# A RoPE attention and two local-attention layers on one core: the norm's factor and offset move from the weights into ScalarE's copies, and the layer weights are prepared in pieces in earlier passes

## The chip, the cores and the metric

The kernel runs on one core of one Trainium2 chip. The metric is the device time of one execution in microseconds (us). The engines are TensorE (PE, with its weight loads as PEld), VectorE (DVE), ScalarE (ACT), GpSimd (POOL) and SyncE (SP), which here only issues transfers. Each works through its own list of instructions in order and waits on semaphores of the others.

## The reference

x has 8 batches of 512 tokens and 256 features. Its parts, cut to what matters:

```
xn = layernorm(x)                               # no factor, no offset
s  = softmax(causal(rope(xn Wq) rope(xn Wk)^T / 16)) (xn Wv)
for l in (0, 1):                                # on xn
    h = shift_token(x)                          # second half of the features, one token later
    q, k, v = split(h @ wqkv[l])                # 256 -> 3 x 512, 8 heads of 64
    q, k = l2norm(q) * qs, l2norm(k) * ks       # then rotary with xpos scales
    x = x + local_attention(q, k, v, window 128) @ wo[l]
    h = shift_token(x)
    h = (h - mean) / sqrt(var + 1e-5) * g[l] + b[l]
    a, gate = split(h @ w1[l] + b1[l])          # 256 -> 2 x 682
    x = x + (a * gelu(gate)) @ w2[l] + b2[l]
out = x_in + s * silu(x)
```

## The kernel before

All products are made of fp32r parts: a number is written as hi (what ACT's copy rounds it to) and lo (the rest, a subtraction on DVE or POOL), and a product is three: hi·hi, hi·lo, lo·hi. So weights must be prepared: class `W` holds for wqkv, w1, wo and w2 a staging buffer, a `_hi` and a `_lo`, and functions `high_*` (ACT) and `low_*`. In the kernel before, the norm's factor g is multiplied into w1 when hi and lo are made (`high_w1`, `low_w1`), and the offset b goes through w1 in `b1_products`, 44 one-column products on PE, whose sum `b1_columns` adds to the bias b1.

`attention_block` does the first attention in 9 software-pipelined steps: step i projects and rotates batch i (front) and does softmax and values of batch i−1 (back). Steps 1 to 6 are one hardware loop; 0, 7 and 8 are written out, and step 8 has only the back. The queue of SP loads batch i+1 (L309), stores the result of the step (L314), loads the layers' weights but w1 in step 0 and w1 in step 7, into the room of the rotation tables `a_tables`. In step 8 ACT and DVE prepare layer 0's weights (L149 to L189), POOL scales the layers' rotation tables (L329) and PE does `b1_products` (L197). L210 is the end of the block, at which all engines meet.

`layers_block` has 17 passes. Pass i does the attention part of one batch and the feed-forward part (ffn) of the batch before: pass 0 attention only, 1 to 7 in layer 0, 8 the turn (attention in layer 1, ffn in layer 0), 9 to 15 in layer 1, 16 ffn and the final products with x and s. The order of the work in a pass is written out by hand for each engine. PE projects four tiles of q, k, v (L1245) with the norm's mean and variance between them (L1252, L1256), then alternates products of the hidden layer (`hidden`, L1271) with transposes of q and k (L1293), then scores (L1310), transposes of the weights (L1324), values (L1340), `down` (L1281) and the output product (L1358). ACT squares projected tiles (L876), makes the inverse norms (L881, L883), f_hi (`high_f`, L962), gelu (L910) and the exponentials (L943). DVE rotates (L1048, L1054), sums squares (L1058, L1060), multiplies the gate (L1068), copies k's transposes out of PSUM (`k_evac`, L1124) and makes maxima (L1104); it adds the attention's result to x at the end (L1222) and starts the norm (L1228, L1229). POOL makes f_lo (`low_f`, L834), the squares and scaled tiles (L812, L819) and h_lo (L823).

In the turn, layer 1's weights are prepared: wqkv at the end of pass 7, the rest in pass 8, with `b1_products` at unit 9 of its attention; PE waits for all low parts of wqkv at the start of pass 8 and for the others at its end.

## Time and profile before

| | |
|---|---|
| time, median of 3 runs | 1464.69 us (1464.49 to 1465.24) |
| profiled execution | 1466.16 us, span of instructions 1464.4 us |
| granted clock of TensorE, mean | 0.983 |
| PE busy | 1397.7 us, 95% |
| DVE / ACT / POOL busy | 66% / 58% / 52% |
| chain that ended last | PE 72%, ACT 6%, issue 3% |

The stretches, read from the windows: start and steps of the attention block to 191.3 us, its last step and end to 216.8, pass 0 to 280.4, passes 1 to 6 to 729.1, pass 7 to 804.8, pass 8 to 891.2, passes 9 to 15 to 1415.1, pass 16 to 1464.4. A time in a row is in us from the span's start; the number behind it is the length, and brackets at a row's end give how long the engine was idle before and what released it.

### The profile page before, as it was taken

The page shows a single profiled execution, that of the slowest core. Times are in us where ns is not written, and L with a number is a line of the kernel's source. Part 1 is how long each engine was busy: PE and PEld are TensorE (multiplying, and loading weights), DVE is VectorE, ACT ScalarE, POOL GpSimd, SP SyncE. Part 2 cuts the span into 40 slices and gives each one's busy share as a digit, 9 for nine tenths or more (in the row PEclk, how much of TensorE's full clock was granted, in tenths as well). Part 3 has the DMA queues.
Part 4 walks back from the last instruction along what each step waited for, and adds up shares of the span by engine and source line. Part 5 has one row for each costly group of instructions (what it writes and reads, how often), then busy time and mean ns, then how long its engine had stood idle before and what let it go on. Part 6 is the DMA issues. An engine that isn't in the chain of part 4 may idle for free.

```text
span 1464.4 us, 24262 instructions
## 1 busy us (share of the span) xinstructions
PE 1397.7 (95%) x7828; PEld 1066.0 (73%) x7828; DVE 961.4 (66%) x2664; ACT 853.1 (58%) x2175; POOL 754.2 (52%) x514
## 2 busy tenths in 40 slices
PE   5999978999999999999999999999999999999987
PEld 5778766677777777777776767777777777777766
DVE  5767657666666666667576767676766666666666
ACT  3555555564646465656566574747474747565763
POOL 2333336383837373737474643747373738383810
PEclk9999989999999999999999999999999999999998
DMA  7111020000000000000001010000000000000037
GB/s 213 30 57 52 20 68 1 1 1 1 0 0 0 0 0 0 0 0 0 0 1 46 14 59 1 1 0 0 0 0 0 0 0 0 0 0 0 0 106 238
DMA packets 35239, 33.28 MB, mean 23 GB/s; under 512 B 8364, under 2 KB 32896, under 8 KB 35200
## 3 DMA queue, kind: packets, MB, share of 16 engines
q1 hardware_dynamic: 35200, 32.79, 7.0%
q8 instruction: 21, 0.34, 0.1%
q14 instruction: 18, 0.15, 0.0%
HBM read 24.39 MB, written 8.39 MB: 22 GB/s over the span
## 4 chain that ended last, share of the span: by engine, by line
PE 72%; ACT 6%; issue 3%; DVE 1%; POOL 1%; DMA 1%; ACTq 0%; SPq 0%; DVEq 0%; POOLq 0%
PE l_psF L1271 9%; PE l_ring L1245 9%; PE l_psP L1245 9%; PE l_ring L1271 7%; PE l_ring L1340 7%; PE l_psP L1324 7%; PE l_psF L1358 6%; PE l_psS L1281 5%; ACT l_att L943 4%; PE l_psS L1293 4%; PE l_psF L1310 4%; PE l_ring L1281 2%; PE l_psS L1310 2%; PE l_psF L1252 1%; PE l_psF L1256 1%
## 5 line engine op out<-in xcount | busy, mean ns | idle before, releaser
L812 POOL TENSOR_TENSOR l_att<-l_att 128x1024 f32<-128x1024 f32 x64 | 154.1, 2408 | 322.6 <-DVE l_att L1054 322.6
L859 POOL TENSOR_TENSOR l_att<-l_att,l_rinv 128x1024 f32<-128x1024 f32 x64 | 121.2, 1894 | 66.9 <-DVE l_rinv L1111 66.0
L923 ACT ACTIVATE l_att<-l_psP 128x384 f32<-128x384 f32 (+1 forms) x128 | 70.2, 548 | 130.5 <-PE l_psP L1324 130.5
L828 POOL TENSOR_TENSOR l_u_lo<-l_att,l_u_hi 128x512 fp32r<-128x512 f32 x90 | 115.4, 1291 | 58.2 <-ACT l_u_hi L918 58.2
L1116 DVE COPY l_att<-l_psP 128x384 f32<-128x384 f32 (+1 forms) x128 | 78.8, 616 | 85.5 <-PE l_psP L1324 85.2
L1324 PE MATMUL l_psP<-ident,l_att 128*128 128x128 f32 x896 | 125.2, 280 | 2.2 <-DVE l_att L1116 1.5
L1324 PEld LDWEIGHTS l_psP<-ident,l_att 128*128 128x128 f32 x896 | 99.2, 142 | 32.1 <-issue 30.0
L819 POOL TENSOR_TENSOR l_att<-l_att,l_rn 128x1024 f32<-128x1024 f32 x64 | 121.6, 1913 | 0.0
L943 ACT ACTIVATE l_att<-l_psF,l_nb 128x256 f32<-128x256 f32 x256 | 117.8, 483 | 0.0
L1104 DVE CUSTOM_DVE_ANT_0 l_psF<-l_psF,w_mask 128x256 f32<-128x256 f32 x256 | 101.0, 455 | 24.2 <-issue 24.2
L1340 PE MATMUL l_ring<-l_att 128*64 128x256 f32 (+1 forms) x1024 | 111.5, 360 | 1.4 <-ACT l_att L923 1.4
L943 ACT ACTIVATE l_att<-l_psS,l_nb 128x128 f32<-128x128 f32 (+1 forms) x256 | 104.6, 431 | 3.2 <-DVE l_nb L1104 2.8
L1340 PEld LDWEIGHTS l_ring<-l_att 128*64 128x64 f32 x1024 | 68.2, 137 | 51.7 <-issue 17.6
L1068 DVE SCALAR_TENSOR_TENSOR l_att<-l_psF,w_b,l_att 128x512 f32<-128x512 f32 x45 | 33.8, 750 | 108.2 <-ACT l_att L910 108.2
L1104 DVE CUSTOM_DVE_ANT_0 l_psS<-l_psS,w_mask 128x128 f32<-128x128 f32 (+1 forms) x256 | 83.4, 386 | 19.6 <-issue 19.6
L876 ACT ACTIVATE l_att<-l_ring 128x512 f32<-128x512 f32 x64 | 38.1, 596 | 96.6 <-PE l_ring L1245 96.6
L340 POOL TENSOR_TENSOR a_t<-a_raw,a_tables 128x256 f32<-128x256 f32 x32 | 29.4, 917 | 121.9 <-ACT a_raw L355 121.9
L1245 PE MATMUL l_psP<-w_wq_hi,l_hhi 128*128 128x512 f32 x192 | 87.8, 457 | 0.0
L1245 PE MATMUL l_ring<-w_wq_hi,l_hhi 128*128 128x512 f32 x192 | 77.0, 401 | 7.6 <-POOL l_hlo L823 6.6
L1271 PE MATMUL l_psF<-l_fhi,w_w_hi 128*128 128x512 f32 x192 | 80.7, 421 | 0.0
L1310 PE MATMUL l_psF<-l_att 64*128 64x256 f32 x512 | 71.5, 398 | 9.6 <-ACT l_att L943 9.3
L1058 DVE TENSOR_REDUCE l_ssq<-l_att 128x16 f32<-128x1024 f32 x64 | 77.2, 1206 | 0.0
(203 smaller groups left out, 4064.3 us busy)
## 6 DMA issues: line engine op xcount, KB each, us to landing
a_tables<-in_x SPq DMA_DIRECT2D x8, 512.0 KB, 4.2
scratch_s<-a_o SPq DMA_DIRECT2D x8, 512.0 KB, 3.0
l_att<-in_x SPq DMA_DIRECT2D x8, 512.0 KB, 8.7
l_att<-scratch_s SPq DMA_DIRECT2D x8, 512.0 KB, 9.7
out_dram<-l_att SPq DMA_DIRECT2D x7, 512.0 KB, 6.3
aw_stage<-in_wqkv SPq DMA_DIRECT2D x2, 768.0 KB, 7.5
l_att<-in_wqkv SPq DMA_DIRECT2D x2, 768.0 KB, 5.2
w_w_raw<-in_w SPq DMA_DIRECT2D x2, 640.0 KB
```

The lines of the kernel that those rows point to most:

```text
L812: pool.tensor_tensor(rot[:, t, :], rot[:, t, :], t2[t % 2], ALU.add).then_inc(S["added"], 1)
L819: pool.tensor_tensor(r, r, along(rn[:, t, :], DH), ALU.mult).then_inc(S["rot_done"], 1)
L828: pool.tensor_tensor(U_lo[0:rows, j, :], gate_of(j, attn)[0:rows, :], U_hi[0:rows, j, :].bitcast(F32), ALU.subtract).then_inc(S["u_lo"], 1)
L859: pool.tensor_tensor(pr, pr, along(inv, 2 * P), ALU.mult).then_inc(S["p_done"], 1)
L943: last = act.activation(Pr[u % 3][:, g * 2 * P + c0:(g + 1) * 2 * P], ps[:, g * 2 * P + c0:(g + 1) * 2 * P], ACT.Exp, bias=nb[:, u % 3, g: ...
L1104: last = dve.tensor_tensor_reduce(out=block, in0=block, in1=maskT[:, c0:2 * P], scale=1.0, scalar=3e38, op0=ALU.add, op1=ALU.min, accum_ou ...
L1245: last = pe.matmul(proj_of[(3 * t + c) % 4], a[:, k, t * P:(t + 1) * P], w[:, k, c * INNER:(c + 1) * INNER], start=(m == 0), stop=(m == 3 ...
L1271: last = pe.matmul(hidden_of[j % 2][bank], w[:, k, tile * P:(tile + 1) * P], a[:, k, :], start=(m == 0), stop=(m == 3 * KD - 1))
L1281: last = pe.matmul(down_of[c], w[:, k, c * P:(c + 1) * P], u[:, k, :], start=(k == 0 and m == 0), stop=(k == HT - 1 and m == 2))
L1310: last = pe.matmul(ps[:, par * 512 + tt * 2 * P + c0:par * 512 + (tt + 1) * 2 * P], QT[rows, pair, t * P:(t + 1) * P], KT[rows, pair, max( ...
L1324: last = pe.transpose(psP[:, dst:dst + P], Pr[u % 3][:, src:src + P], ident[:, :])
L1340: last = pe.matmul(ring[pair % 2][rows, t * P:t * P + w], V[:, t, h * DH:(h + 1) * DH], PT[:, par, t * 2 * P:t * 2 * P + w], start=(t == 0 ...
```

## The change

- The norm's factor and offset are no longer in the weights. ACT makes f_hi in two Identity instructions of 128x512 with a factor and an offset per partition (`high_f`), and two more write the same value over its input in place (`affine`), from which f_lo is subtracted. `b1_products` and `b1_columns` are gone; b1 is loaded where it is used.
- In `hidden(i, 0)` the eight products that need f_hi alone come first, for both tiles, and the four with f_lo behind them. In the other calls the f_lo products are the last two of each tile.
- Layer 0's w1 has a buffer of its own and is loaded in step 0 with wqkv, both ahead of w2. wqkv is prepared in three pieces in step 6, w1 and wo in step 7, w2 in step 8; high parts on ACT, low parts of wqkv and w1 on DVE, of wo and w2 on POOL. POOL's table products (L329) move from step 8 to step 6, which is written out.
- In the turn wqkv is prepared in three pieces by columns, `high_wo` and `low_wo` at units 4 and 5, `low_w1` behind the last `o_low`, `low_w2` behind the start of the norm. PE waits for a part where it first uses it.

```diff
-    def high_wqkv(self, act, layer, stage, k):
-        act.wait_ge(self.S[f"wq_in{k}"], 16 * (layer + 1))
-        act.activation(self.wq_hi[:, k, :], stage[:, k, :], ACT.Copy).then_inc(self.S["wq_hi"], 1)
+    def high_wqkv(self, act, layer, stage, c):
+        for k in range(KD):
+            act.wait_ge(self.S[f"wq_in{k}"], 16 * (layer + 1))
+        cols = slice(c * INNER, (c + 1) * INNER)
+        act.activation(self.wq_hi[:, :, cols], stage[:, :, cols], ACT.Copy).then_inc(self.S["wq_hi"], 1)
 
     def high_w1(self, act, layer, stage, k):
         act.wait_ge(self.S["w1_in"], 64 * (layer + 1))
-        act.wait_ge(self.S["small"], self.SMALL)
-        act.activation(self.w1_hi[:, k, :], stage[:, k, :], ACT.Copy, scale=self.gcol[:, layer, k:k + 1]).then_inc(self.S["w1_hi"], 1)
-
-
-    def low_wqkv(self, dve, layer, stage, k):
-        dve.wait_ge(self.S["wq_hi"], KD * layer + k + 1)
-        dve.tensor_tensor(self.wq_lo[:, k, :], stage[:, k, :], self.wq_hi[:, k, :].bitcast(F32), ALU.subtract).then_inc(self.S["wq_lo"], 1)
+        act.activation(self.w1_hi[:, k, :], stage[:, k, :], ACT.Copy).then_inc(self.S["w1_hi"], 1)
+
+
+    def low_wqkv(self, dve, layer, stage, c):
+        dve.wait_ge(self.S["wq_hi"], 3 * layer + c + 1)
+        cols = slice(c * INNER, (c + 1) * INNER)
+        dve.tensor_tensor(self.wq_lo[:, :, cols], stage[:, :, cols], self.wq_hi[:, :, cols].bitcast(F32), ALU.subtract).then_inc(self.S["wq_lo"], 1)
 
     def low_w1(self, dve, layer, stage, k):
         dve.wait_ge(self.S["w1_hi"], KD * layer + k + 1)
-        dve.scalar_tensor_tensor(out=self.w1_lo[:, k, :], in0=stage[:, k, :], scalar=self.gcol[:, layer, k:k + 1],
-                                 in1=self.w1_hi[:, k, :].bitcast(F32), op0=ALU.mult, op1=ALU.subtract).then_inc(self.S["w1_lo"], 1)
-
+        dve.tensor_tensor(self.w1_lo[:, k, :], stage[:, k, :], self.w1_hi[:, k, :].bitcast(F32), ALU.subtract).then_inc(self.S["w1_lo"], 1)
...
-            with e.Fori(1, B - 1) as i:
+            with e.Fori(1, B - 2) as i:
                 step(i, True, True)
+            step(B - 2, True, True)
             step(B - 1, True, True)
             step(B, False, True)
...
+                sp.wait_ge(S["w_tr"], 3)
+                W.load_wqkv(sp, 0, stage_q)
+                W.load_w1(sp, 0, stage1)
                 sp.wait_ge(WS["w2pad"], 1)
                 W.load_w2(sp, 0)
-                sp.wait_ge(S["w_tr"], 3)
-                W.load_wqkv(sp, 0, stage_q)
...
-                if isinstance(i, int) and i == B - 1:
-                    W.load_w1(sp, 0, stage1)
...
-                else:
+                if isinstance(i, int) and i == B - 2:
                     layer_tables()
+                if isinstance(i, int) and i == B - 1:
+                    W.low_wo(pool, 0)
+                if isinstance(i, int) and i == B:
+                    W.low_w2(pool, 0)
...
+            def prepare(i, part):
+
+                if isinstance(i, int) and i == B - 2:
+                    W.high_wqkv(act, 0, stage_q, part)
+                if isinstance(i, int) and i == B - 1:
+                    if part < KD:
+                        W.high_w1(act, 0, stage1, part)
+                    else:
+                        W.high_wo(act, 0)
+                if isinstance(i, int) and i == B and part == 0:
+                    W.high_w2(act, 0)
...
-                if not front:
-                    W.high_wqkv(act, 0, stage_q, 1)
+                prepare(i, 0)
...
-                if not front:
-                    for k in range(KD):
-                        W.high_w1(act, 0, stage1, k)
-                    W.high_wo(act, 0)
-                    W.high_w2(act, 0)
...
-                if not front:
-                    for k in range(KD):
-                        W.low_wqkv(dve, 0, stage_q, k)
+                if front:
+                    rotate(i, 2)
+                    rotate(i, 3)
+                if isinstance(i, int) and i == B - 2:
+                    for c in range(3):
+                        W.low_wqkv(dve, 0, stage_q, c)
+                if isinstance(i, int) and i == B - 1:
                     for k in range(KD):
                         W.low_w1(dve, 0, stage1, k)
-                    W.low_wo(dve, 0)
-                    W.low_w2(dve, 0)
-                    W.b1_columns(dve, 0, psT)
-                if front:
-                    rotate(i, 2)
-                    rotate(i, 3)
...
-                if not front:
-                    W.b1_products(pe, 0, stage1, psT)
...
                 def low_f():
-                    ge(pool, S["f_hi"], i)
+                    ge(pool, S["affine_done"], i)
                     pool.tensor_tensor(flo[:, :, :], dF, fhi[:, :, :].bitcast(F32), ALU.subtract).then_inc(S["f_lo"], 1)
...
                 def high_f():
                     ge(act, S["hn_done"], i)
-                    act.activation(fhi[:, :, :], dF, ACT.Copy).then_inc(S["f_hi"], 1)
+                    for k in range(KD):
+                        last = act.activation(fhi[:, k, :], dF[:, k], ACT.Identity, scale=W.gcol[:, lf, k:k + 1], bias=W.bcol[:, lf, k:k + 1])
+                    last.then_inc(S["f_hi"], 1)
+
+                def affine():
+                    for k in range(KD):
+                        last = act.activation(dF[:, k], dF[:, k], ACT.Identity, scale=W.gcol[:, lf, k:k + 1], bias=W.bcol[:, lf, k:k + 1])
+                    last.then_inc(S["affine_done"], 1)
...
-                    if turn and j == TT:
-                        W.high_wo(act, 1)
...
+                        if turn and u == 4:
+                            W.high_wo(act, 1)
                         if turn and UNITS <= u < UNITS + KD:
                             W.high_w1(act, 1, stage1, u - UNITS)
                         if last and u == UNITS + 3:
-                            for k in range(KD):
-                                W.high_wqkv(act, 1, stage, k)
+                            for c in range(3):
+                                W.high_wqkv(act, 1, stage, c)
...
-                    W.low_wo(dve, 1)
...
-                        if turn and UNITS <= u < UNITS + KD:
-                            W.low_w1(dve, 1, stage1, u - UNITS)
+                        if turn and u == 5:
+                            W.low_wo(dve, 1)
...
                 if last:
+                    for c in range(3):
+                        W.low_wqkv(dve, 1, stage, c)
+                if turn:
                     for k in range(KD):
-                        W.low_wqkv(dve, 1, stage, k)
-                if turn:
-                    W.low_w2(dve, 1)
+                        W.low_w1(dve, 1, stage1, k)
                 if attn:
                     ge(dve, S["wo_ps"], i + 1)
                     for k in range(KD):
                         xk = xT[:, bass.ds(i - B * la, 1), k * X1:k * X1 + N]
                         dve.tensor_tensor(xk, xk, psF[:, k * N:(k + 1) * N].unsqueeze(1), ALU.add).then_inc(S["x_attn"], 1)
-                    if turn:
-
-                        W.b1_columns(dve, 1, psS[:, N:2 * N])
                     ge(dve, S["x_attn"], KD * (i + 1))
                     h = h_view(xT, i - B * la)
                     dve.tensor_tensor(rstdF[:, :].unsqueeze(1), h[:, 0:1, :], h[:, 1:2, :], ALU.add).then_inc(S["h_sum"], 1)
                     dve.tensor_scalar(dF, h, 1.0, None, ALU.mult).then_inc(S["h_ready"], 1)
+                if turn:
+                    W.low_w2(dve, 1)
...
                     m, of = 0, 3 * t + c - 4
+                    if fresh is not None:
+                        pe.wait_ge(WS["wq_lo"], 3 * fresh + c + 1)
...
             def hidden(i, j, attn):
                 u = i - 1
-                ge(pe, S["f_lo"], i)
+                ge(pe, S["f_hi"], i)
...
+                terms = [(k, w, fhi) for k in range(KD) for w in (w1_hi, w1_lo)] + [(k, w1_hi, flo) for k in range(KD)]
                 tiles = ((HFULL + j, 0), (j, 1)) if j < HFULL else ((2 * HFULL, 0),)
-                for tile, bank in tiles:
-                    m = 0
-                    for k in range(KD):
-                        for w, a in ((w1_hi, fhi), (w1_lo, fhi), (w1_hi, flo)):
-                            last = pe.matmul(hidden_of[j % 2][bank], w[:, k, tile * P:(tile + 1) * P], a[:, k, :], start=(m == 0), stop=(m == 3 * KD - 1))
-                            m += 1
+                for wanted in (("hi", "lo") if j == 0 else ("hi lo",)):
+                    if wanted != "hi":
+                        ge(pe, S["f_lo"], i)
+                    for tile, bank in tiles:
+                        for n, (k, w, a) in enumerate(terms):
+                            if ("lo" if a is flo else "hi") in wanted:
+                                last = pe.matmul(hidden_of[j % 2][bank], w[:, k, tile * P:(tile + 1) * P], a[:, k, :],
+                                                 start=(n == 0), stop=(n == 3 * KD - 1))
...
-                if turn:
-                    pe.wait_ge(WS["wq_lo"], KD * LAYERS)
-                if attn:
-                    project(i, 0)
+                if attn:
+                    project(i, 0, la if turn or not ffn else None)
...
+                if ffn:
+                    pe.wait_ge(WS["w1_lo"], KD * (lf + 1))
...
+                    pe.wait_ge(WS["w2_lo"], lf + 1)
...
-                        if turn and u == UNITS + 1:
-                            W.b1_products(pe, 1, stage1, psS[:, N:2 * N])
-                    if turn:
-                        pe.wait_ge(WS["wo_lo"], LAYERS)
+                    pe.wait_ge(WS["wo_lo"], la + 1)
                     output(i, range(0, 1))
                     values(i, PAIRS - 1, ffn)
                     output(i, range(1, PAIRS))
-                    if turn:
-                        pe.wait_ge(WS["w1_lo"], KD * LAYERS)
-                        pe.wait_ge(WS["w2_lo"], LAYERS)
```

ACT in an ordinary pass, from the third projected tile on. Before (L892 copies v, L962 is `high_f`, L876 squares the fourth tile):

```order
L892 ACTIVATE l_att<-l_ring 128x512
L962 ACTIVATE l_fhi<-l_ffn 128x1024
L41 ISA
L876 ACTIVATE l_att<-l_ring 128x512
L881 ACTIVATE l_lnq<-l_lnq 128x16
L883 ACTIVATE l_rn<-l_lnq 128x16
L41 REGISTER_ALU
```

And now (L951 is `high_f`, L956 `affine`):

```order
L880 ACTIVATE l_att<-l_ring 128x512
L951 ACTIVATE l_fhi<-l_ffn,w_b,w_g 128x512 x2
L956 ACTIVATE l_ffn<-l_ffn,w_b,w_g 128x512 x2
L41 ISA
L864 ACTIVATE l_att<-l_ring 128x512
L869 ACTIVATE l_lnq<-l_lnq 128x16
L871 ACTIVATE l_rn<-l_lnq 128x16
L41 REGISTER_ALU
```

Between the copy of v and the fourth square stand four instructions where one stood.

DVE at the end of step 6 and the beginning of step 7, now (L486 and L489 rotate, L160 is `low_wqkv`, L494 takes maxima, L479 and L480 write the low part and the copy of x):

```order
L486 TENSOR_TENSOR a_rot<-a_raw,a_tables 128x512
L489 TENSOR_TENSOR a_rot<-a_rot,a_t 128x512
L486 TENSOR_TENSOR a_rot<-a_raw,a_tables 128x512
L489 TENSOR_TENSOR a_rot<-a_rot,a_t 128x512
L160 TENSOR_TENSOR w_wq_lo<-aw_stage,w_wq_hi 128x2x512 x3
L494 TENSOR_REDUCE a_nb<-a_psS 128x1
L479 TENSOR_TENSOR a_hlo<-a_ring,a_hhi 128x512 x2
L480 COPY xT<-a_ring 128x512
L494 TENSOR_REDUCE a_nb<-a_psS 128x1
```

Before, the rotations of the loop's last step were followed by the maxima, and DVE's preparation stood at the very end of the block:

```order
L500 RECIPROCAL a_rinv<-a_sums 128x1
L505 COPY a_pt<-a_psP 128x512
L159 TENSOR_TENSOR w_wq_lo<-aw_stage,w_wq_hi 128x1536 x2
L163 SCALAR_TENSOR_TENSOR w_w_lo<-a_tables,w_g,w_w_hi 128x1408 x2
L173 TENSOR_TENSOR w_wo_lo<-w_wo_raw,w_wo_hi 128x1024
L189 TENSOR_TENSOR w_w_lo<-w_w_raw,w_w_hi 128x1536
L202 TENSOR_TENSOR w_b<-a_psT,w_b1raw 128x11
```

POOL now, in step 6 and step 7 (L327 and L328 are its part of the rotation, L316 the table products, L172 `low_wo`, L188 `low_w2`):

```order
L327 TENSOR_TENSOR a_t<-a_raw,a_tables 128x256
L328 TENSOR_TENSOR a_t<-a_raw,a_tables 128x256
L316 TENSOR_TENSOR w_cos<-w_cos,a_scl 128x512
L316 TENSOR_TENSOR w_sin<-w_sin,a_scls 128x512
L316 TENSOR_TENSOR w_cos<-w_cos,a_scl 128x512
L316 TENSOR_TENSOR w_sin<-w_sin,a_scls 128x512
L327 TENSOR_TENSOR a_t<-a_raw,a_tables 128x256
L328 TENSOR_TENSOR a_t<-a_raw,a_tables 128x256
```

The table products stood behind the last such pair of step 7 before; now they stand between those of step 6 and step 7.

DVE at the end of pass 8, before (L163 is `low_w1`, L189 `low_w2`, L202 `b1_columns`):

```order
L163 SCALAR_TENSOR_TENSOR w_w_lo<-l_ffn,w_g,w_w_hi 128x1408
L1116 COPY l_att<-l_psP 128x512
L1120 TENSOR_TENSOR l_ot_lo<-l_ring,l_ot_hi 128x512
L1083 SCALAR_TENSOR_TENSOR xT<-l_psS,w_b,xT 128x512
L1120 TENSOR_TENSOR l_ot_lo<-l_ring,l_ot_hi 128x512
L189 TENSOR_TENSOR w_w_lo<-w_w_raw,w_w_hi 128x1280
L189 TENSOR_TENSOR w_w_lo<-w_w_raw,w_w_hi 42x256
L1222 TENSOR_TENSOR xT<-xT,l_psF 128x512 x2
L202 TENSOR_TENSOR w_b<-l_psS,w_b1raw 128x11
L1228 TENSOR_TENSOR l_ffn<-xT 128x512
L1229 TENSOR_SCALAR l_ffn<-xT 128x1024
```

And now (L164 is `low_w1`, L188 `low_w2`):

```order
L1117 TENSOR_TENSOR l_ot_lo<-l_ring,l_ot_hi 128x512
L1080 SCALAR_TENSOR_TENSOR xT<-l_psS,w_b,xT 128x512
L1117 TENSOR_TENSOR l_ot_lo<-l_ring,l_ot_hi 128x512
L164 TENSOR_TENSOR w_w_lo<-l_ffn,w_w_hi 128x1408 x2
L1219 TENSOR_TENSOR xT<-xT,l_psF 128x512 x2
L1222 TENSOR_TENSOR l_ffn<-xT 128x512
L1223 TENSOR_SCALAR l_ffn<-xT 128x1024
L188 TENSOR_TENSOR w_w_lo<-w_w_raw,w_w_hi 128x1280
L188 TENSOR_TENSOR w_w_lo<-w_w_raw,w_w_hi 42x256
```

The two of w1 moved from among the units to directly before the addition to x, and those of w2 from before it to behind the start of the norm.

## Rows read from the trace of the kernel before

**Rows 1.** The page: busy time of each engine.

```profile
PE 1397.7 (95%) x7828; PEld 1066.0 (73%) x7828; DVE 961.4 (66%) x2664; ACT 853.1 (58%) x2175; POOL 754.2 (52%) x514
```

**Rows 2.** Windows: stretch, length, busy by engine, granted clock, DMA share, GB/s.

```profile
280.40:729.10 448.70, 442.74 (x2510) 334.31 (x2509) 293.53 (x870) 269.45 (x714) 259.13 (x168) 1.00 0.00 0
729.10:804.80 75.70, 73.69 (x418) 55.32 (x417) 52.20 (x148) 47.50 (x121) 43.18 (x28) 1.00 0.06 22
804.80:891.20 86.40, 83.41 (x463) 64.72 (x463) 56.05 (x151) 49.99 (x124) 43.48 (x28) 0.94 0.10 31
```

**Rows 3.** Chain of waits of one ordinary pass: start, length, what.

```profile
376.73 0.87 PE l_psS L1293 x8
...
380.40 0.91 PE l_psS L1293 x8
```

**Rows 4.** Timeline of ACT in that pass: start, length, instruction, [idle before].

```profile
370.08 1.05 ACT L962 ACTIVATE l_fhi<-l_ffn 128x1024 fp32r<-128x1024 f32 x1
...
371.03 0.58 ACT L876 ACTIVATE l_att<-l_ring 128x512 f32<-128x512 f32 x1
```

**Rows 5.** Timeline of DVE in that pass.

```profile
355.40 1.28 DVE L1222 TENSOR_TENSOR xT<-xT,l_psF 128x512 f32 x2 [3.17 <-PE l_psF L1358]
...
372.70 0.69 DVE L1048 TENSOR_TENSOR l_att<-l_ring,w_cos 128x512 f32<-128x512 f32 x1
...
376.47 0.19 DVE L1060 TENSOR_REDUCE l_lnq<-l_ssq 128x16 f32<-128x32 f32 x1
...
379.86 0.68 DVE L1124 COPY l_att<-l_psS 128x512 f32<-128x512 f32 x1
```

**Rows 6.** Timeline of POOL in that pass.

```profile
371.21 2.41 POOL L834 TENSOR_TENSOR l_flo<-l_ffn,l_fhi 128x1024 fp32r<-128x1024 f32 x1 [0.56 <-ACT l_fhi L962]
...
380.15 3.79 POOL L819 TENSOR_TENSOR l_att<-l_att,l_rn 128x1024 f32<-128x1024 f32 x2
```

**Rows 7.** Groups by form on ACT: busy us, mean ns of one.

```profile
L956 ACT ACTIVATE l_ffn<-l_psF,eps 128x512 f32<-128x512 f32 x16 | 11.0, 688 | 4.1 <-PE l_psF L1256 4.1
...
L958 ACT ACTIVATE l_psF<-l_ffn 128x512 f32<-128x512 f32 x16 | 9.6, 602 | 0.5
...
L918 ACT ACTIVATE l_u_hi<-l_att 128x512 fp32r<-128x512 f32 x75 | 46.7, 622 | 0.4
```

**Rows 8.** Windows around the arrival of x(2).

```profile
28.00:36.00 8.00, 7.96 (x50) 7.67 (x50) 2.85 (x5) 4.59 (x10) 2.52 (x2) 0.73 0.99 357
```

**Rows 9.** Timeline of DVE and of PE where attention step 6 ends and 7 begins.

```profile
165.43 0.69 DVE L491 TENSOR_TENSOR a_rot<-a_rot,a_t 128x512 f32<-128x512 f32 x1
...
170.49 0.29 DVE L496 TENSOR_REDUCE a_nb<-a_psS 128x1 f32<-128x128 f32 x1 [4.37 <-PE a_psS L619]
...
171.89 0.68 DVE L482 COPY xT<-a_ring 128x512 f32<-128x512 f32 x1
...
173.02 0.48 PE L600 MATMUL a_ring<-aw_hi,a_hhi 128*128 128x512 f32 x1
```

**Rows 10.** Timeline of DVE and of POOL at the end of step 7.

```profile
187.67 1.66 DVE L491 TENSOR_TENSOR a_rot<-a_rot,a_t 128x512 f32<-128x512 f32 x1
...
191.67 1.26 POOL L329 TENSOR_TENSOR w_sin<-w_sin,a_scls 128x512 f32<-128x512 f32 x1
```

**Rows 11.** Timeline of PE, and SyncE's waits, at the attention block's end.

```profile
203.50 6.70 PE L197 MATMUL a_psT<-w_b,a_tables 128*128 128x1 f32 x44
...
SPq L210 <- PEq L210: 4.8, 1, 4.8
```

**Rows 12.** Timeline of PE and of DVE in pass 8.

```profile
873.11 7.23 PE L197 MATMUL l_psS<-w_b,l_ffn 128*128 128x1 f32 x44
...
889.01 1.82 DVE L189 TENSOR_TENSOR w_w_lo<-w_w_raw,w_w_hi 128x1280 fp32r<-128x1280 f32 x2 [0.77 <-ACT w_w_hi L183]
```

**Rows 13.** Timeline of DVE and of PE in the last pass.

```profile
1429.21 1.22 DVE L1155 TENSOR_TENSOR l_flo<-l_ffn,l_fhi 128x1024 fp32r<-128x1024 f32 x1 [1.12 <-ACT l_fhi L962]
...
1429.81 1.09 PE L1350 MATMUL l_psP<-ident,xT 128*128 128x128 f32 x4 [3.13 <-ACT xT L928]
```

47 lines of the change are left out of this document (15 added, 32 removed).

## The prediction

> **What bounds the kernel now.** I read the page first: TensorE (PE) is busy for 95% of the span [rows 1], so time comes only from shortening the stretches in which it is not, or from PE work that goes away. The windows then say where those are [rows 2]. Six ordinary passes of the layers take 448.70 us, 74.78 each, at granted clock 1.00, with PE busy but for 1 us a pass. Pass 7 takes 75.70 and pass 8, in which the layer changes, 86.40 at a mean clock of 0.94: together 162.1 where two ordinary passes take 149.6, so the turn costs 12.5. The third place is the end of the attention block, where 44 one-column products take 6.70 and the block closes after them [rows 11].
>
> The chain of an ordinary pass is nearly all PE, so the question for each edit there is how much room the engines beside it have. I followed the place where the new ScalarE (ACT) work goes. There ACT writes f_hi (L962), then squares the fourth projection tile (L876) [rows 4]; VectorE (DVE) has by then worked without a gap since 355.40 and takes that square up at 372.70, goes on without a gap to the reduction at 376.47, behind which ACT does a logarithm, an exponential, a table load and the first gelu; DVE multiplies with it and then copies k's first bank, 379.86 to 380.54 [rows 4, 5]. PE's second block of transposes, which writes that bank again from its middle on, takes 0.91 where the block before took 0.87 [rows 3]. So this side chain ends just in time: PE already waits a few hundredths for it. A delay of its head has no slack behind it, only the one in front of it.
>
> **The norm's factor and offset.** f_hi was one copy of 128x1024 and becomes two Identity instructions of 128x512 with two pointer operands, with two more behind them (in place, for f_lo). All four stand ahead of the square. Successive instructions overlap by 0.10 (1.05 long, next one 0.95 later [rows 4]). The same shape costs 0.60 without a pointer and 0.69 with one, a plain copy in SBUF 0.62 [rows 7]. No row has two pointers. Bounds: the second costs nothing (pitch 0.62 + 0.09 − 0.10 = 0.61) or as much as the first (0.70). I take 0.70, since the only measured step is that of one more pointer. Then the square starts at 370.08 + 4 × 0.70 = 372.88, ends 0.58 later, and DVE begins at about 373.50 instead of 372.70: 0.80 late. As the chain behind has no slack, the pass grows by 0.80. With 0.61 the square ends at 373.10 and the delay is 0.44 (0.40 without the handover). Passes 1 to 7 and 10 to 15 are of this kind: **13 × 0.80 = +10.4** (low end +5.7). The new order of the first hidden products (eight that need f_hi alone, then four with f_lo) takes away no wait: f_lo starts about 1.8 later (373.0 instead of 371.21 [rows 6]) and ends at 375.4, when those four come up.
>
> The Trainium skill bears on the missing row (ScalarE: Activation LUTs, What ACT_TABLE_LOAD costs): an ACTIVATE takes 186 ns plus 0.833 per column, about 93 more for each [128,1] pointer operand, and neighbours overlap by about 93. The rows agree for one pointer (602 to 688 [rows 7]); no row here shows the second. By the page the pitch is an estimated 0.70 and the sum stays; were the second free, it would be 4.7 lower.
>
> The last pass has no projection to hide behind. There PE waits 3.13 for ACT's copies of xT behind f_hi [rows 13]. The four instructions take 2.80 where one took 0.95: **+1.85**.
>
> **The turn.** Gone are the 44 products in pass 8 (7.23 [rows 12]), the half-speed products that followed them, the wait for all of wqkv's low parts at the pass's start, and low_wo, which held DVE's maxima back. I take the whole excess: **−12.5**, the low end being the products alone, −7.2. Against this: pass 8 has the 0.80 too, and DVE enters it late, because PE no longer waits for low_wqkv but DVE still does it first; the two delays overlap on ACT, and I take **+1.05** for both. low_wo at the sixth unit: 0.05. In pass 8 DVE now does low_w1 in the 3.17 that it idles before adding to x [rows 5]: twice 1.22 × 1408/1024 [rows 13], 3.4, hidden but for 0.2. Behind the norm's first copies it does low_w2, 1.82 for its two instructions [rows 12], ahead of the first rotation of pass 9; DVE has no gap from there, so pass 9 is later by that, with the variance's chain in front: **+1.87**, in place of its 0.80.
>
> **The attention block.** Step 6's end gets POOL's four table products and DVE's three pieces of low_wqkv. DVE is free from 166.12 (165.43 + 0.69) to 170.49 [rows 9], and a 128x1024 subtraction takes 1.22 alone [rows 13], so three would take 3.66 and fit. But POOL reads SBUF at the same time. In step 7 of before a DVE rotation beside these very table products took 1.66 [rows 10] instead of 0.69 [rows 9], and POOL's product 1.26 when alone [rows 10], 1.3 with its start. If they alternate, three of POOL's lie between DVE's: 166.12 + 3.66 + 3.9 = 173.7, so the maxima of step 7 start 3.2 late, and with them the low parts and the copy of x at 171.89, on which PE's first projection waits; that copy ended at 172.57 and the projection came at 173.02 [rows 9], so 0.4 is slack: **+2.8**, from 0 (no alternation) to 3.5.
>
> The Trainium skill says the same of the port (SBUF — State Buffer, Who interferes with whom): a DVE instruction with two SBUF inputs and a GpSimd instruction that reads SBUF lock each other out for a whole instruction. The trace agrees (1.66 for 0.69). Without the lock the sum would be 2.8 lower.
>
> At step 7's end low_wo on POOL meets the last rotations in the same way: **+0.9** (a rotation grew by 0.97 [rows 9, 10]). ACT, busy for 58% of the span [rows 1], gets up to three copies a step there, and I count them as hidden between its evacuations. In step 8 high_w2 and low_w2 lie beside PE's work. At the close, SyncE last waits 4.8 for PE [rows 11], before that for the store; with the 44 products gone the store decides: **−4.8**. At the start 1.4 MB of w1 now go ahead of x(2), 3.9 us at the 357 GB/s of that stretch [rows 8]; x(2) was in before its use by about that much: **+0.1**, at most 1.5.
>
> **Sum:** 0.1 + 2.8 + 0.9 − 4.8 + 10.4 − 12.5 + 1.05 + 0.05 + 1.87 + 1.85 = +1.7. Against the profiled execution, 1466.16 with a span of 1464.4, that is 1467.9; the median of the three timed runs is 1464.69, so the time is forecast as **1466.4**. A measurement of this kernel can tell some 0.2%, 2.9 us, from no change; this is the same.
>
> **Rivals.**
> - *The second pointer is free.* Nothing in the trace is against it. 13 passes at 0.44, the last pass at 1.5: 1466.4 − 4.7 − 0.4 = 1461.3, and less if low_f lands sooner. 15 in 100.
> - *The square's delay is covered.* If PE's wait at the transposes is not DVE's, or the delay is caught up between reduction and gelu, the passes cost nothing: −10.4, 1456. For it: that wait is only 0.04. Against it: no gap on DVE and ACT from the square to the copy. 12 in 100.
> - *The lock doesn't alternate.* DVE's three pieces run back to back: 1466.4 − 2.8 = 1463.6. 10 in 100.
> - *Slower: POOL's chain becomes the bound.* All of POOL's products behind f_lo move by 1.8. The third scaled tile ends at 380.15 + 1.9 = 382.1 [rows 6], so at 383.9 after, and the third block of transposes comes at 384.0 plus PE's own delay of 0.8. Under 0.9 of slack decides; each 0.3 over it costs 13 × 0.3 = 4: 1470.5. 10 in 100.
> - *Slower: the block doesn't close sooner*, because the store, or POOL's low_w2 behind low_wo, ends as late as PE did: 1466.4 + 4.8 = 1471.2. 8 in 100.
> - My forecast: 45 in 100, its own range 1464 to 1469.
>
> **Numbers.** The range 1459 to 1470.5 leaves out most of the covered case and the upper end of the two slower ones. Under 1461.8 counts as faster, over 1467.6 as slower: faster 0.27 (the covered case, more than half of the free pointer, a little of the forecast), slower 0.31 (both slower cases and a quarter of the forecast, whose terms of the turn can be short by up to 5), same 0.42.
>
> **What would show it.** Ordinary passes at 75.6 instead of 74.78, at clock 1.00; the four Identity instructions at a pitch of 0.70; DVE idle for 0.8 before L1045, the rotation of the fourth tile; PE's wait at the second block of transposes grown to 0.8. Step 7's first projection 2.8 later, with stretched subtractions on DVE between POOL's table products. The block's end waiting for the store. Passes 7 and 8 together at about 151.4, with clock 1.00. The prediction falls if the passes stay at 74.8 or if the turn keeps a wait of several us on a low part that is now later.

## The result, and the profile after

The changed kernel takes 1468.29 us (median of 20 runs, 1465.75 to 1469.85) beside 1465.01 for the kernel before (20 runs, 1463.06 to 1466.46): ratio 1.0021, interval 1.0015 to 1.0028. The forecast was 1466.4, a change too small to be told from none. The measured change is small, but its interval leaves out 1: by the forecast's own bounds (over 1467.6 is slower) it fell on the slower side, to which the forecast gave 0.31, and "same" 0.42. The profiled execution took 1468.67, its span 1466.8.

The page: busy times, and the chain by engine and line.

```profile
PE 1387.9 (95%) x7740; PEld 1050.2 (72%) x7740; DVE 963.1 (66%) x2662; ACT 878.2 (60%) x2225; POOL 761.7 (52%) x516
...
PE 59%; ACT 12%; DVE 8%; issue 5%; POOL 1%; ACTq 0%; DVEq 0%; POOLq 0%
```

PE works 10 us less than in [rows 1], and the span is 2.4 longer. ACT and DVE now hold 20% of the chain. The windows of passes 1 to 6, of pass 7 and of pass 8, after:

```profile
281.16:733.68 452.52, 443.92 (x2509) 333.80 (x2508) 293.72 (x870) 278.91 (x732) 258.92 (x168) 1.00 0.00 0
733.68:809.10 75.42, 73.99 (x419) 55.62 (x418) 51.09 (x147) 49.10 (x125) 43.17 (x28) 1.00 0.06 22
809.10:885.61 76.51, 74.32 (x419) 55.72 (x418) 54.41 (x151) 51.36 (x127) 43.17 (x28) 1.00 0.11 36
```

An ordinary pass takes 75.42 us (452.52 / 6) where it took 74.78; the turn's two passes take 151.9 where they took 162.1 [rows 2]. In the ordinary pass, the timelines of ACT, DVE, POOL and PE (lines between are left out at each ...):

```profile
371.40 1.51 ACT L951 ACTIVATE l_fhi<-l_ffn,w_b,w_g 128x512 fp32r<-128x512 f32 x2
372.82 1.51 ACT L956 ACTIVATE l_ffn<-l_ffn,w_b,w_g 128x512 f32<-128x512 f32 x2
374.23 0.58 ACT L864 ACTIVATE l_att<-l_ring 128x512 f32<-128x512 f32 x1
```

```profile
374.84 0.69 DVE L1045 TENSOR_TENSOR l_att<-l_ring,w_cos 128x512 f32<-128x512 f32 x1 [0.62 <-ACT l_att L864]
...
382.00 0.68 DVE L1121 COPY l_att<-l_psS 128x512 f32<-128x512 f32 x1
```

```profile
374.40 2.41 POOL L822 TENSOR_TENSOR l_flo<-l_ffn,l_fhi 128x1024 fp32r<-128x1024 f32 x1 [2.25 <-ACT l_ffn L956]
```

```profile
376.46 0.40 PE L1272 MATMUL l_psF<-l_fhi,w_w_lo 128*128 128x512 f32 x1
376.87 1.20 PE L1272 MATMUL l_psF<-l_flo,w_w_hi 128*128 128x512 f32 x4
...
381.93 0.63 PE L1294 MATMUL l_psS<-ident,l_att 128*128 128x128 f32 x4 [0.18 <-ACT l_att L889]
382.83 0.63 PE L1294 MATMUL l_psS<-ident,l_att 128*128 128x128 f32 x4 [0.27 <-DVE l_att L1121]
```

Pitch here is the time from one start to the next. The four instructions have a pitch of 0.71, the square starts 2.83 behind their start, and DVE idles 0.62 before it takes it. At the other end of the chain PE waits 0.18 for ACT's copy of q at the start of the second transposes and 0.27 for DVE's copy of k at their middle (4 of 8 stand before it). It also waits about 0.2 for f_lo, whose first product comes 0.41 behind the one before, where 0.23 is the pitch: POOL starts f_lo 17.8 after the pass's first product (356.59), before 16.1 (371.21 [rows 6], 355.09).

The end of step 6 in DVE and POOL, and PE:

```profile
166.41 6.71 DVE L160 TENSOR_TENSOR w_wq_lo<-aw_stage,w_wq_hi 128x1024 fp32r<-128x1024 f32 x3
173.05 0.28 DVE L494 TENSOR_REDUCE a_nb<-a_psS 128x1 f32<-128x128 f32 x1
```

```profile
167.59 2.25 POOL L316 TENSOR_TENSOR w_cos<-w_cos,a_scl 128x512 f32<-128x512 f32 x1
```

```profile
173.96 2.34 PE L608 MATMUL a_psS<-a_qk 128*128 128x384 f32 x4 [2.75 <-ACT a_p L368]
```

The window that follows it:

```profile
176.20:178.20 2.00, 2.00 (x8) 1.67 (x7) 0.82 (x3) 0.67 (x2) 0.00 (x0) 0.56 0.00 0
```

Three subtractions of 1.22 took 6.71, and each of the two POOL products beside them 2.25 instead of 1.26. The maxima came at 173.05, 0.65 ahead of the forecast 173.7. PE idled 2.75, and behind that its granted clock was 0.64 from 173.90 to 176.20 and 0.56 to 178.20, so partly at the lower of the two levels, before it was 1.00 again; the products of 128x512 in there came every 0.43 to 0.57, where the pitch at full clock is 0.23. The end of the block:

```profile
194.52 0.66 PE L599 MATMUL a_psP<-ident,a_rot 128*128 128x128 f32 x4 [1.19 <-DVE a_rot L489]
...
207.17 1.97 PE L625 MATMUL a_psO<-a_v,a_pt 128*128 128x256 f32 x8 [0.66 <-ACT a_o L376]
217.76 0.77 PE L1243 MATMUL l_ring<-w_wq_hi,l_hhi 128*128 128x512 f32 x1 [8.63 <-POOL l_hlo L811]
```

PE's last values end at 209.14 instead of 203.66, and pass 0 starts 8.62 behind them instead of 13.10.

### The profile page after: what moved, and what is told of

Read it like the earlier page. It is cut to its first block, busy times and chain, and to the rows that moved or that the text cites. A ratio compares the mean times of both kernels' runs of the same rounds, so it can differ in the third digit from the quotient of the medians.

```text
span 1466.8 us, 24159 instructions
## 1 busy us (share of the span) xinstructions
PE 1387.9 (95%) x7740; PEld 1050.2 (72%) x7740; DVE 963.1 (66%) x2662; ACT 878.2 (60%) x2225; POOL 761.7 (52%) x516
## 4 chain that ended last, share of the span: by engine, by line
PE 59%; ACT 12%; DVE 8%; issue 5%; POOL 1%; ACTq 0%; DVEq 0%; POOLq 0%
PE l_ring L1341 7%; PE l_ring L1243 7%; PE l_psP L1325 6%; PE l_psF L1272 6%; PE l_psF L1359 6%; PE l_psP L1243 5%; PE l_ring L1272 5%; PE l_psS L1282 5%; PE l_psF L1311 3%; ACT l_att L931 3%; PE l_psS L1294 3%; PE l_ring L1282 2%; PE l_psS L1311 2%; ACT l_fhi L951 2%; DVE l_att L1051 2%
## 5 line engine op out<-in xcount | busy, mean ns | idle before, releaser
L1101 DVE CUSTOM_DVE_ANT_0 l_psS<-l_psS,w_mask 128x128 f32<-128x128 f32 (+1 forms) x256 | 83.6, 387 | 19.3 <-issue 19.3
L327 POOL TENSOR_TENSOR a_t<-a_raw,a_tables 128x256 f32<-128x256 f32 x32 | 29.8, 933 | 118.1 <-ACT a_raw L346 118.1
L1294 PE MATMUL l_psS<-ident,l_att 128*128 128x128 f32 x512 | 69.7, 274 | 11.0 <-ACT l_att L889 5.1
```

The costliest lines, as they stand in the source:

```text
L1101: last = dve.tensor_tensor_reduce(out=block, in0=block, in1=maskT[:, c0:2 * P], scale=1.0, scalar=3e38, op0=ALU.add, op1=ALU.min, accum_ou ...
L1294: last = pe.transpose(psS[:, j * 512 + a * P:j * 512 + (a + 1) * P], rot[:, t, j * INNER + a * P:j * INNER + (a + 1) * P], ident[:, :])
```

## The experiments

Each run is set beside the kernel before, with runs of both on the same chip (4 to 10 executions of the edited kernel); ratios are to the kernel before, with 95% intervals. Its median was 1465.0 to 1465.3 in every series, so times are also compared with the changed kernel's 1468.29. All kernels but those that say so are edits of the changed one. The edits are cut to the lines that matter.

**1. The four instructions without pointers.** `ACT.Copy` without scale and bias in `high_f` and `affine`, so that the norm's factor and offset are left out:

```diff
-last = act.activation(fhi[:, k, :], dF[:, k], ACT.Identity, scale=W.gcol[...], bias=W.bcol[...])
+last = act.activation(fhi[:, k, :], dF[:, k], ACT.Copy)
```

> The changed kernel with plain copies in place of the four Identity instructions (no factor and no offset is applied, so the norm's output lacks both). Theory A, ScalarE's four instructions delay the fourth square and through it the rotation, the gelu and the second block of transposes: the pitch falls from 0.71 to about 0.53 us, the square comes 0.7 earlier, VectorE's idle 0.62 before the fourth rotation is gone, and an ordinary pass takes about 74.8 instead of 75.42; over 13 passes, pass 8, 9 and the last pass about 9.5 us less than the changed kernel, near 1459. Theory B, the growth of the pass comes from the late low part (PE's wait at the first hidden products) and from the new order of these products: the pass loses at most the 0.28 of that wait and stays above 75.1.

1458.47, ratio 0.9953 (0.9936 to 0.9969). The timeline of ACT in an ordinary pass:

```profile
371.54 1.14 ACT L951 ACTIVATE l_fhi<-l_ffn 128x512 fp32r<-128x512 f32 x2
372.58 1.14 ACT L956 ACTIVATE l_ffn<-l_ffn 128x512 f32<-128x512 f32 x2
373.62 0.59 ACT L864 ACTIVATE l_att<-l_ring 128x512 f32<-128x512 f32 x1
```

The pitch is 0.52, DVE no longer idles, and passes take 74.77, with the order of the first hidden products as in the changed kernel. Theory A holds, B does not.

**2. One pointer.** The norm's offset is left out.

```diff
-last = act.activation(fhi[:, k, :], dF[:, k], ACT.Identity, scale=W.gcol[...], bias=W.bcol[...])
+last = act.activation(fhi[:, k, :], dF[:, k], ACT.Identity, scale=W.gcol[...])
```

> The changed kernel with the factor alone in the four Identity instructions (the norm's offset is left out). Theory A with the second pointer operand costing as much as the first: pitch 0.62, the square 0.36 earlier, a pass of 75.07, total about 5 us less than the changed kernel. Rival, the second pointer is free and the first costs 0.18 or Identity is slower than a copy: pitch stays 0.71 and the pass stays at 75.42.

1462.13, ratio 0.9982 (0.9972 to 0.9992):

```profile
371.35 1.33 ACT L951 ACTIVATE l_fhi<-l_ffn,w_g 128x512 fp32r<-128x512 f32 x2
372.58 1.32 ACT L956 ACTIVATE l_ffn<-l_ffn,w_g 128x512 f32<-128x512 f32 x2
373.80 0.58 ACT L864 ACTIVATE l_att<-l_ring 128x512 f32<-128x512 f32 x1
```

The pitch is 0.61, and passes take 75.03. So the pitches are 0.52, 0.61 and 0.71 (means over all passes 0.521, 0.613 and 0.706): each pointer costs 0.09, the second as much as the first (the first step also goes from Copy to Identity). The rival of the free second pointer is out.

**3. GpSimd's products in step 8.**

```diff
-                if isinstance(i, int) and i == B - 2:
-                    layer_tables()
-                if isinstance(i, int) and i == B - 1:
-                    W.low_wo(pool, 0)
                 if isinstance(i, int) and i == B:
+                    W.low_wo(pool, 0)
+                    layer_tables()
                     W.low_w2(pool, 0)
```

> The changed kernel with GpSimd's table products and its low part of wo moved to step 8 of the attention block (before the low part of w2); VectorE's pieces stay. Theory A, the lock between VectorE and GpSimd made the stall: the three subtractions of wqkv take 3.7 instead of 6.71 us, PE's wait of 2.75 in step 7 and the half-speed products after it are gone, and the 1.19 before the last transposes too; pass 0 starts 5 to 6 us earlier, at about 212.2, total about 5.5 less. Rival, the extra copies on ScalarE or VectorE's pieces alone are enough to hold the maxima back: at most 2 us come back. Second rival, GpSimd ends later than the store in step 8 and the gain is lost to the block's end.

1466.71, ratio 1.0011 (1.0001 to 1.0020): 1.6 less than the changed kernel, not the expected 5.5. DVE, and PE's waits there:

```profile
165.52 3.49 DVE L160 TENSOR_TENSOR w_wq_lo<-aw_stage,w_wq_hi 128x1024 fp32r<-128x1024 f32 x3
...
187.28 2.75 DVE L487 TENSOR_TENSOR a_rot<-a_rot,a_t 128x512 f32<-128x512 f32 x1
189.95 5.30 DVE L164 TENSOR_TENSOR w_w_lo<-aw_stage,w_w_hi 128x1408 fp32r<-128x1408 f32 x2
```

```profile
PE a_psS L606 <- ACT a_p L366: 2.5, 1, 2.5
PE a_psP L597 <- DVE a_rot L487: 1.2, 1, 1.2
```

The three subtractions of wqkv take 3.49 alone, so the wait in step 7 is gone. But nothing in these products waits for step 8: POOL had run ahead into step 7, and the lock moved to the rotation (2.75) and to low_w1 (5.30). The experiment had not taken the lock away (lock: VectorE and GpSimd instructions that hold each other up).

**4. The same, behind a wait for low_w1.**

```diff
                 if isinstance(i, int) and i == B:
+                    pool.wait_ge(WS["w1_lo"], KD)
                     W.low_wo(pool, 0)
                     layer_tables()
```

> The changed kernel with GpSimd's low part of wo, table products and low part of w2 in step 8, and now behind a wait for VectorE's low parts of w1, so that no product of GpSimd's overlaps a subtraction or a rotation of VectorE (in the run before, GpSimd ran ahead into step 7 and the lock only moved there). Theory A, the lock is all of it: the subtractions of w1 take 3.3 instead of 5.30 us, PE's waits of 1.18 and 2.46 at the end of step 7 and in step 8 are gone, pass 0 starts near 212, total about 5.5 below the changed kernel, near 1462.8. Rival, VectorE's low parts of w1 alone are too long for the gap before step 8's maxima: 1 to 2 us of wait stay. Second rival, GpSimd's later products end behind the store and hold the block's end.

1462.40, ratio 0.9982 (0.9972 to 0.9991), 5.9 below the changed kernel:

```profile
187.92 0.69 DVE L488 TENSOR_TENSOR a_rot<-a_rot,a_t 128x512 f32<-128x512 f32 x1
188.53 3.15 DVE L164 TENSOR_TENSOR w_w_lo<-aw_stage,w_w_hi 128x1408 fp32r<-128x1408 f32 x2
191.93 0.29 DVE L493 TENSOR_REDUCE a_nb<-a_psS 128x1 f32<-128x128 f32 x1 [0.25 <-PE a_psS L608]
```

low_w1 takes 3.15, the rotation 0.69, the maxima wait for PE only, and pass 0 starts at 212.25 instead of 217.76. Steps 7 and 8 take as long as in the kernel before (34.7 from step 7's first transposes to the last values, before 35.0), so the lock was all of the stall.

**5. The places of the buffers.** An unused buffer of 88 bytes a partition, where the raw b1 lay before.

```diff
+        self.b1raw = sb("b1raw", [P, LAYERS, W1T])
         self.b1col = sb("b1", [P, LAYERS, W1T])
```

> The changed kernel with an unused buffer of 88 bytes per partition where the raw b1 lay before, so that all later buffers lie where they lay in the kernel before (as far as the first block's new staging buffer does not move them). It asks why the projection's products came every 0.230 us instead of 0.2333 before. Theory: their pitch depends on where the operands lie; it returns to 0.2333, the projection takes 0.17 longer, the norm's copies start later against the pass, and the ordinary pass grows to about 75.6, total +2.5. Rival: placement has nothing to do with it; pitch and pass stay at 0.230 and 75.42.

1471.17, ratio 1.0039 (1.0025 to 1.0054). DVE's rotation of the fourth tile, and the first twelve products of the projection in the chain, here and then in the changed kernel:

```profile
372.95 0.69 DVE L1046 TENSOR_TENSOR l_att<-l_ring,w_cos 128x512 f32<-128x512 f32 x1 [0.79 <-ACT l_att L865]
```

```profile
354.69 2.80 PE l_ring L1244 x12
```

```profile
356.75 2.76 PE l_ring L1243 x12
```

The twelve take 2.80 as in the kernel before, DVE idles 0.79 instead of 0.62, and a pass takes 75.57 (the changed one 75.42). So the move of buffers that came with the removal of b1raw was worth 0.15 a pass, and without it the growth is 75.57 − 74.77 = 0.80, the forecast's number.

**6. v's copy behind the fourth squares.**

```diff
                 if attn:
-                    evacuate(i, 2)
+                    evacuate(i, 2, () if ffn else (2,))
                 if ffn:
                     high_f()
                     affine()
                 if attn:
-                    evacuate(i, 3)
+                    evacuate(i, 3, (2, 3) if ffn else (3,))
```

The third argument lists the tiles whose v is copied, behind the squares; without it only the tile's own is.

> The changed kernel with one move on ScalarE: the copy of the third tile's v goes behind the fourth tile's squares, so that the four Identity instructions start when the norm is ready (0.18 us after the square before them) and not behind the projection of v. Theory A, only the end of these four against VectorE's need of the fourth square counts: the square comes 1.0 us earlier, VectorE doesn't idle before the fourth rotation, PE waits neither for the low part nor at the second transposes; an ordinary pass takes 74.6 (74.77 less the 0.17 of the faster projection), total about 10.5 below the changed kernel, near 1458. Rival, the late copy of v becomes the new wait (PE's second hidden tile needs all of v) or the pass has another bound behind at 75.0 or more.

1458.97, ratio 0.9949 (0.9932 to 0.9965). ACT and DVE:

```profile
369.20 1.53 ACT L955 ACTIVATE l_fhi<-l_ffn,w_b,w_g 128x512 fp32r<-128x512 f32 x2 [0.20 <-DVE l_ffn L1145]
370.63 1.51 ACT L960 ACTIVATE l_ffn<-l_ffn,w_b,w_g 128x512 f32<-128x512 f32 x2
372.04 0.58 ACT L864 ACTIVATE l_att<-l_ring 128x512 f32<-128x512 f32 x1
```

```profile
372.85 0.19 DVE L1061 TENSOR_REDUCE l_lnq<-l_ssq 128x16 f32<-128x32 f32 x1
373.02 0.69 DVE L1049 TENSOR_TENSOR l_att<-l_ring,w_cos 128x512 f32<-128x512 f32 x1
```

ACT waits 0.20 for the norm and starts the four at once. The square ends at 372.62, DVE is busy until 373.02 and doesn't wait. Passes take 74.80, not the expected 74.6: with ACT's delay gone PE still waits 0.27 for the copy of k at the second transposes, so the pass is bound by the same just-in-time chain as before, and the faster projection brings nothing.

**7. The kernel before without the 44 products**, and without `b1_columns`; b1 is loaded where it is used, and the norm's offset is left out. In both blocks:

```diff
-                if not front:
-                    W.b1_products(pe, 0, stage1, psT)
...
-                        if turn and u == UNITS + 1:
-                            W.b1_products(pe, 1, stage1, psS[:, N:2 * N])
```

> The kernel before with one part of the change alone: the 44 one-column products and the addition to b1 are gone in both layers, nothing else moves (the norm's offset is left out). Theory A of the prediction: the attention block closes when the store has landed, 4.8 us earlier, and the turn loses 7.2 of products and the slower clock behind them, about 9.3 of the 12.5 of excess; the waits for the low parts of wqkv and for VectorE's low part of wo, 3.2, stay. Total about 14 less than before, near 1451. Rival: low parts on VectorE, in step 8 after step 7, and in pass 8, become the new bound once the products are gone; the block gains 2 or less and the turn 7.2 or less, total near 1456.

1457.65, ratio 0.9942 (0.9925 to 0.9958). DVE at the end of the block, SyncE's wait, and the window of pass 8:

```profile
209.54 1.75 DVE L189 TENSOR_TENSOR w_w_lo<-w_w_raw,w_w_hi 128x1536 fp32r<-128x1536 f32 x1
211.76 0.48 DVE L1031 MEMSET l_ffn<- 128x512 f32 x1 [0.46 <-PEq L210]
```

```profile
SPq L210 <- PEq L210: 4.7, 1, 4.7
```

```profile
804.60:884.21 79.61, 75.48 (x418) 56.84 (x419) 56.12 (x151) 50.00 (x124) 43.50 (x28) 0.98 0.10 34
```

Pass 8 takes 79.61 instead of 86.4: the products, with what they did to the granted clock (0.94 over pass 8 before, 0.98 here), were worth 6.7. The block's end gained 0.1: last values to pass 0 is 13.0 us still. PE idles there now, and DVE's low_w2 runs to 211.29, 8.0 behind the last values; in the kernel before DVE's work ended 8.1 behind them, at 211.73. So the wait that the profile puts down to PE's queue (4.7 here too, with no work of PE) was the meeting of all engines, and DVE came last. The rival held. Dropping the products did not close the block by itself. Moving the low parts alone was not run; since the 44 products of the kernel before ended at 210.20, it could have given 1.5 by estimate (211.73 − 210.20). The 4.5 took both.

**8. The kernel before, moved by 40 bytes.**

```diff
+        self.gap = sb("gap", [P, 10])
         self.b1col = sb("b1", [P, LAYERS, W1T])
```

> The kernel before with an unused buffer of 40 bytes per partition before b1, which moves all later buffers by 40 bytes, modulo 128 the same as the 88 bytes that the change takes away. Theory, a place modulo 64 or 128 bytes sets the pitch of the projection's products: it falls from 0.2333 to 0.2295, 48 products a pass save 0.18, and as in the changed kernel nothing else moves; a pass of 74.6, total about 2.7 less. Rival: the pitch hangs on an absolute place (or on the first block's buffers), and neither pitch nor time changes.

1464.84, ratio 0.9994 (0.9985 to 1.0004), pass 74.85. The pitch is not lower; the theory of a place modulo 128 falls.

**9. The kernel before, moved by 32 bytes**: `sb("gap", [P, 8])` in the same place.

> The kernel before with an unused buffer of 32 bytes per partition before b1. The projection's moving operand l_hhi then lies at 181728 instead of 181696; in the changed kernel it lies at 181600, in the run with 40 bytes (rounded to 64) at 181760. Theory left over from the last runs: a place 32 bytes past a multiple of 64 gives the pitch of 0.2295, a multiple of 64 gives 0.233 or 0.234; so 0.2295 here. A pass stays at about 74.7, since VectorE's chain to the second transposes bounds it and not the projection (the run with v's copy moved had the faster pitch and 74.80 a pass): total -1 to 0. Rival: the pitch hangs on the distance to some other buffer or on the program's own order, and stays at 0.233.

1462.13, ratio 0.9981 (0.9972 to 0.9990). Passes 1 to 6 in one window:

```profile
278.79:726.09 447.30, 441.27 (x2509) 334.39 (x2508) 293.78 (x870) 269.53 (x714) 259.42 (x168) 1.00 0.00 0
```

A pass takes 74.55, and the projection's pitch is as before (2.80 for twelve), so this theory falls too; the hidden and output products got faster, from 0.233 to 0.230. Where operands lie is worth 0.2 us a pass, and no rule for it was found.

**10. Three moves together:** experiments 4 and 6, and in the last pass `silu(10)` and `silu(11)` ahead of `high_f`:

```diff
                     act.preload_act_table_set(SILU)
+                    for n in range(10, 12):
+                        silu(n)
                     high_f()
                     affine()
-                    for n in range(10, 14):
+                    for n in range(12, 14):
```

> The changed kernel with three moves together: GpSimd's preparation late in step 8, ScalarE's copy of v behind the fourth squares, and in the last pass two silu copies (10 and 11), for which PE waited 4.77, ahead of the norm's four instructions. By the first two alone 1468.3 - 5.9 - 9.3 = 1453.1; the last pass gains 2 to 2.5 if PE's wait for the copies was its bound, 0 if the hidden products or VectorE's final products hold its end: 1450.6 to 1453.

1452.01, ratio 0.9914 (0.9901 to 0.9928), 16.3 below the changed kernel. PE's wait for ACT's copies in the last pass is no longer 4.77:

```profile
1412.93 0.63 PE L1356 MATMUL l_psP<-ident,xT 128*128 128x128 f32 x4 [2.54 <-ACT xT L919]
```

Behind it PE now waits 0.68 for f_hi. The third move brought about 1 and not the expected 2 to 2.5, since the other two alone add up to 1453.1.

**11. low_w2 of the turn on GpSimd**, in the kernel of experiment 10, behind its last product of pass 8: `low_w2(dve, 1)` is gone from `step` on VectorE, and on GpSimd

```diff
+                if attn and ffn and la != lf:
+                    W.low_w2(pool, 1)
```

> As the kernel with three moves, and in the turn the low part of w2 goes from VectorE, ahead of the first rotation of pass 9, to GpSimd behind its last product of pass 8, where it idles for 18 us. Theory: the 1.2 to 1.5 that pass 9 takes over an ordinary pass is VectorE's 1.81 for these two instructions and goes away; VectorE loses at most one product's length to the lock. Total 1.2 to 1.5 below the kernel with three moves. Rival: GpSimd's 3.4 us lock out VectorE's low parts of w1 and the norm's start just then, and pass 8 or 9 pays as much.

1452.02, ratio 0.9917 (0.9903 to 0.9931): nothing gained. DVE and POOL:

```profile
870.67 5.92 DVE L164 TENSOR_TENSOR w_w_lo<-l_ffn,w_w_hi 128x1408 fp32r<-128x1408 f32 x2
```

```profile
871.78 5.41 POOL L188 TENSOR_TENSOR w_w_lo<-w_w_raw,w_w_hi 128x1280 fp32r<-128x1280 f32 x2 [9.58 <-ACT w_w_hi L182]
```

DVE's low_w1 takes 5.92 instead of 3.15. The rival was right: the lock took back more than the move gave, and pass 9 takes 77.2 instead of 76.3 (that the times are equal comes from pass 1, which started 0.6 earlier in this profile).

**12. k's first copy before the first gate product**, in the kernel of experiment 11.

```diff
                 for j in range(HT):
+                    if attn and j == 0:
+                        k_evac(i, j)
                     if ffn:
                         gated(i, j, lf, attn)
-                    if attn and j < TT:
+                    if attn and 0 < j < TT:
                         k_evac(i, j)
```

> As the last kernel, and on VectorE the first copy of k's transposes goes before the first gate product (it is ready at 377.3 in the profile of before, while VectorE idles 2.53 until the gelu). Theory: the just-in-time chain table load, gelu, gate, copy, second transposes is what bounds an ordinary pass at 74.77; without it the pass takes PE's own time, some 0.2 to 0.4 less, 15 passes 3 to 6 us less. Rival: the wait only moves to the copy of q or to the next gate product, and the pass stays at 74.8.

1445.75, ratio 0.9870 (0.9855 to 0.9885). DVE in an ordinary pass, and passes 1 to 6:

```profile
372.92 0.69 DVE L1128 COPY l_att<-l_psS 128x512 f32<-128x512 f32 x1 [0.53 <-PE l_psS L1301]
374.92 0.75 DVE L1072 SCALAR_TENSOR_TENSOR l_att<-l_psF,w_b,l_att 128x512 f32<-128x512 f32 x1 [1.31 <-ACT l_att L903]
```

```profile
276.52:722.32 445.80, 440.01 (x2510) 334.68 (x2508) 294.27 (x870) 279.42 (x732) 258.95 (x168) 1.00 0.00 0
```

The copy fills DVE's idle time ahead of the gelu, PE no longer waits at the second transposes, and a pass takes 74.30 instead of 74.77: 6.3 less than experiment 11. This is the fastest version, 19.3 below the kernel before.

## Why the prediction was right

The stages of the two profiles, beside the terms of the sum (pass starts and ends as in the chain and the timelines):

| place | forecast | measured |
|---|---|---|
| x(2) later | +0.1 | no wait in this profile; step 7 starts 0.2 earlier (168.47 for 168.68) |
| steps 6 to 8 | +2.8, +0.9 | +5.7 (168.47 to 209.14 instead of 168.68 to 203.66) |
| block's end | −4.8 | −4.5 |
| 13 ordinary passes | 13 × 0.80 = +10.4 | 13 × 0.65 = +8.5 |
| turn, passes 7 and 8 | −12.5 + 1.05 + 0.05 | −11.0 |
| pass 9 | +1.87 | +1.8 |
| last pass | +1.85 | +2.3 |
| sum | +1.7 | +2.4, with −0.2 in pass 0 |

That the sum is within 0.7 is partly luck: the term of the lock was 2.0 too small and that of the ordinary passes 1.9 too large.

*Factor and offset.* The mechanism was right link by link: the pitch (0.71 for 0.70), the late square, DVE's idle time, the late copy, PE's wait at the second transposes; experiments 1, 2 and 6 take the links apart. The sizes of the last links were smaller than forecast: DVE idles 0.62 and not 0.8, PE waits 0.45 at these transposes, and 0.2 of the delay shows already at f_lo, where the forecast saw no wait. The term was too large by 0.15 a pass because buffers moved, which the prediction did not consider; with them back DVE idles 0.79 and the pass grows by 0.80 (experiment 5).

*The lock.* It alternated as forecast, and the maxima came within 0.7 us of the forecast time. Mis-sized was the term for PE, 3.7 for 5.7. The wait was not at the projection but earlier, at the third scores (2.75, for the exponentials behind the maxima), about as long as forecast. Left out was the granted clock behind this wait (0.64 for 2.3 us, 0.56 for 2.0), by estimate 1.7 (2.3 × 0.36 + 2.0 × 0.44) of the 1.8 that the two waits leave over. At the end of step 7 the last rotation took 2.75 instead of 1.66, a wait of 1.19 and not 0.9. Experiment 4 gives all of it back.

*The block's end.* The number was right and the reason wrong, which is luck: "with the 44 products gone the store decides" holds only because the low parts moved too (experiment 7). The misread row is SyncE's wait of 4.8 [rows 11], which is for the meeting of all engines and not for PE's products.

*The turn.* The excess went, nearly all of it; the products were 6.7 of it (experiment 7); in what experiment 7 leaves, PE waits 1.0 for wqkv's low part and 2.5 for an exponential in pass 8. What low_w1 and low_w2 cost in passes 8 and 9 was sized right.

*The last pass* lost 2.3 for 1.85. The four instructions and the copy behind them were sized right (from `high_f` to that copy 2.83 instead of 0.97, 1.86 more). The rest lies before them, in the two products of the norm's variance; now and before:

```profile
1424.01 2.08 PE L1254 MATMUL l_psF<-l_ffn,ones 128*128 128x512 f32 x2 [1.86 <-DVE l_ffn L1135]
```

```profile
1423.92 1.12 PE L1256 MATMUL l_psF<-l_ffn,ones 128*128 128x512 f32 x2 [1.86 <-DVE l_ffn L1138]
```

The granted clock was 0.50 in them now and 1.00 before. It is not the change's: in experiment 4, with the same last pass, they took 1.19 at 1.00, and in experiment 8, whose last pass is that of the kernel before, they took 2.08.

Of the rivals, the free pointer and the covered square are shown wrong by experiments 2 and 1, the lock that doesn't alternate by the changed kernel's own trace and experiment 4; POOL's chain did not become the bound, though its f_lo was 0.2 late; the block did close sooner. The timed change is +3.3 where the two profiles differ by 2.4, mostly because the profiled execution of the kernel before took 1.15 more than its median (1466.16 beside 1465.01) and that of the changed kernel 0.38 more.

## What to carry to other kernels

Before work is put on an engine with idle time, find the place in its order where a result is awaited: ScalarE was 58% busy, and 1.9 us more in front of one square cost 0.65 in each of 13 passes; the same work, started as soon as its input was there and not behind a copy that waits (experiment 6), cost none. Follow a chain that ends just in time back through its engines: one copy moved into an idle gap (experiment 12) was worth 6.3, nearly as much as the 44 products in the turn. Work put on GpSimd is not free for VectorE when both read SBUF (a rotation took 2.75 instead of 0.69, experiments 3 and 4), and an engine without a wait runs ahead, so a move in the code is not a move in time (experiment 3).
